# First layer of a two-layer transformer block: causal mask written by ScalarE into the scores' bank, and probabilities transposed into two PSUM banks by turns

## The chip, the cores and the metric

One core of a Trainium2 chip. The time is the device time of one execution in microseconds (us). The engines are named as in the profile: PE is TensorE (PEld its weight loads), DVE VectorE, ACT ScalarE, POOL GpSimd, SP SyncE, which here only issues DMAs.

## The reference, cut to what matters

Two layers run over x of shape (8, 256, 256); each adds an attention and a feed-forward branch to its input, both computed from the same layer norm. The change is in the first layer's attention, which is causal, with 16 query heads of width 16 and one key and value head:

```python
xn = _layernorm(x, axis=-1)
x = x + _L0_attn_ref(xn, ...) + _L0_ffn_ref(xn, ...)
# in _L0_attn_ref:
scores = jnp.einsum('bqhd,bkd->bhqk', q, k) * scale
causal = jnp.tril(jnp.ones((S, S), dtype=bool))
scores = jnp.where(causal[None, None], scores, min_val)
attn = jax.nn.softmax(scores, axis=-1)
ctx = jnp.einsum('bhqk,bkd->bqhd', attn, v)
```

The second layer has a full attention with 16 heads of width 128 and a mixture of 16 experts. The change does not touch it.

## The kernel before, in words

All work is in float32 held as a high and a low part (`fp32r`), so a product takes three matmuls: high by high, high by low, low by high. ACT writes the high part of a PSUM result, and DVE the low part behind it.

The first layer takes two sequences (512 tokens) at a time, in four turns. The attention of a turn is cut into 24 units, `units[g]`, 96 in all (`ALL`). A unit fills one PSUM bank (128 queries by 512 columns): for the first 128 queries of a sequence (`t` = 0) it holds four heads of 128 keys, and for the second 128 (`t` = 1) two heads of 256 keys. Each engine runs a written-out order of steps, `step(g)`:

- PE: `scores(g)`, `transposes(g-2)`, the items of `early[g]`, shared-expert work of `back_at[g]` (`shared`), `context(g-3)`, the items of `late[g]`. Items are the other products of the layer: `xT`, `q`, `kv`, `ffn`, `ctx`, `out`, `norm`. Here the shared expert belongs to the second layer and is done early.
- DVE: the row maxima of unit g (L791), the low part of the transposed probabilities of unit g-2 (L795), then its share of the items.
- ACT: `high_probs(g-2)` (L510), `exps(g)` (L502), then its share of the items.
- POOL: low parts of the hidden units and contexts, and in every step the splitting of a chunk of the second layer's weights, which SP stores and reloads.

`scores(g)` writes into `ps_s[g % 2]`. It begins with a product of the identity with the mask (L905), which writes minus 1e30 above the diagonal into the diagonal blocks (512 columns for `t` = 0, 256 for `t` = 1); one or two products of queries and keys (L907) are added onto it. It waits for the exponentials of unit g-2, which read the same bank.

`transposes(g)` turns the unit's probabilities in four 128x128 blocks (L916) into the one bank `ps_t`, ACT copies it out (L510), DVE takes the rest (L795), and only then may `transposes(g+1)` write `ps_t` again:

```python
pe.wait_ge(p_ok.sem, p_ok.at(0, g + 1))
pe.wait_ge(t_low.sem, t_low.at(0, g))
```

`context(g)` (L931 to L933) multiplies them with the values and waits for the low part of unit g. The bank `ps_b` serves the shared-expert items alone: ten of them per turn, placed in steps 8 to 16 and 23 of the turn after (in steps 8 to 17 for the third turn's; those of the last turn come behind the 96 steps). The last 18 steps of items are spread into the second layer.

Of the kernel before, what the change touches and what calls it, by code (L numbers as in the profile page):

```python
# [7 lines left out]
F32 = mybir.dt.float32  # L8
# [46 lines left out]
def stage_layer0(nc, ctx, dram):  # L55
# [40 lines left out]
    w_qkv = [sb(f"w_qkv{i}", [P, DC, D + P], R32) for i in range(2)]  # L96
    nc.sbuf_base += 4 * 4 * PC
    parts = [sb(f"parts{i}", [P, 2, PC], R32) for i in range(2)]
# [50 lines left out]
    raw_up = sb("raw_up_l0", [P, DC, HID], I32)  # L149
    mask_f = sb("mask_f", [P, P])  # L150
    assert nc.sbuf_base <= region_probs
# [101 lines left out]
    def stats_of(i):  # L253
        return TP + i

    qkv_parts = [(raw_qkv[:, :, 0:D], [w[:, :, 0:D] for w in w_qkv], HD0 ** -0.5),
                 (raw_qkv[:, :, D:D + P], [w[:, :, D:D + P] for w in w_qkv], 1.0),
# [13 lines left out]
    var_ok = sem("var_ok")  # L271
    zero_ok = sem("zero_ok")
    q3_rest = sem("q3_rest")
    cleared = sem("cleared")
# [144 lines left out]
    def gpsimd(pool):  # L419
        pool.memset(zeros[:], 0.0).then_inc(zero_ok, 1)  # L420
        pool.memset(ident[:], 0.0).then_inc(filled, 1)
        pool.memset(mask_f[:], 0.0).then_inc(filled, 1)
        pool.memset(minus_half[:], -0.5).then_inc(filled, 1)
        pool.wait_ge(filled, 3)
        pool.affine_select(out=ident[:], in_=ident[:], compare_op=ALU.not_equal, fill=1.0, base=0,
                           pattern=[[-1, P]], channel_multiplier=1).then_inc(const_ok, 1)
        pool.affine_select(out=mask_f[:], in_=mask_f[:], compare_op=ALU.is_ge, fill=MASKED, base=0,
                           pattern=[[-1, P]], channel_multiplier=1).then_inc(const_ok, 1)
# [65 lines left out]
    def scalar(act):  # L494
        act.sem_inc(p_ok.sem, 2)

        def exps(g):
# [7 lines left out]
            last.then_inc(p_ok.sem, 1)  # L505

        def high_probs(g):
            act.wait_ge(t_full.sem, t_full.at(0, g + 1))
            act.wait_ge(pv_ok.sem, pv_ok.at(0, g - 1))
            act.activation(pT[0][:, g % 2, :], ps_t[:], ACT.Copy).then_inc(t_high.sem, 1)  # L510

# [54 lines left out]
        for item in front:  # L566
            if item[0] == "q" and item[2] == 0:
                act.wait_ge(const_ok, 2)
                act.activation(ident_r[:], ident[:], ACT.Copy).then_inc(consts_r, 1)
                act.activation(mask_r[:], mask_f[:], ACT.Copy).then_inc(consts_r, 1)  # L570
                act.wait_ge(small_ok, 3)
                act.wait_ge(pads_zero, 2)
            early_item(item)
        def step(g):
# [30 lines left out]
            if LATE_AT <= g < LATE_AT + len(late_parts):  # L605
                raw, (high, _) = late_parts[g - LATE_AT]
                if g == LATE_AT:
                    act.wait_ge(late_in, 16 * LATE_LOADS)
                    act.wait_ge(pads_zero, 3)
                act.activation(high, raw, ACT.Copy).then_inc(late_high, 1)  # L610

        for g in range(ALL):
# [3 lines left out]
    def vector(dve):  # L616
# [170 lines left out]
        def step(g):  # L787
# [5 lines left out]
            if 2 <= g < ALL + 2:  # L793
                dve.wait_ge(t_high.sem, t_high.at(0, g - 1))
                dve.tensor_tensor(pT[1][:, g % 2, :], ps_t[:], pT[0][:, g % 2, :].bitcast(F32), ALU.subtract)\  # L795
                    .then_inc(t_low.sem, 1)
# [46 lines left out]
    def tensor(pe):  # L843
        pe.sem_inc(pv_ok.sem, 2)

        def product3(out, lhs, rhs, start, stop):
# [3 lines left out]
            return last  # L850

        def shared(p, n):

# [7 lines left out]
            if BACK[p][n] == ("sum", 0):  # L861
                pe.wait_ge(hs_low.sem, hs_low.at(0, len(ST) * (p + 1)))
            pe.wait_ge(b_done.sem, b_done.at(0, back_count(p, n) - (p == TURNS - 1 and n > 0)))
            out = back_bank(p, n)
            if kind == "ffs":
# [26 lines left out]
        def scores(g):  # L892
            p, s, t, j, nj = units[g]
            nh, w = DC * nj, (t + 1) * P
            out = ps_s[g % 2]
            if g == 0:
                pe.wait_ge(consts_r, 2)
            if t == 0 and j == 0:
                pe.wait_ge(item_done.sem, item_done.at(0, number["kv", p, s] + 1))
                pe.wait_ge(q3_got[s], 64 * (p + 1))  # L900
            if g == DC_HEADS // 4:
                pe.wait_ge(q3_rest, 64)
            pe.wait_ge(p_ok.sem, p_ok.at(0, g - 1))
            by_head = out[:].rearrange("p (h k) -> p h k", h=nh)
            pe.matmul(by_head[:, :, t * P:w], ident_r[:], mask_r[:].unsqueeze(1).to_broadcast([P, nh, P]), start=True, stop=False, skip_group_check=True)  # L905
            for a in range(nj):
                last = pe.matmul(out[:, a * DC * w:(a + 1) * DC * w].rearrange("p (c k) -> p c k", c=DC),  # L907
                                 q3[:, s, j + a, t * P:(t + 1) * P], k3[:, s, :, 0:w],
                                 start=False, stop=(a == nj - 1), skip_group_check=True)
            last.then_inc(s_full.sem, 1)  # L910

        def transposes(g):
            pe.wait_ge(p_ok.sem, p_ok.at(0, g + 1))
            pe.wait_ge(t_low.sem, t_low.at(0, g))
            for b in range(4):
                last = pe.transpose(ps_t[:, b * P:(b + 1) * P], probs[:, g % 3, b * P:(b + 1) * P], ident[:])  # L916
            last.then_inc(t_full.sem, 1)
# [1086 lines left out]
```

## Time and profile before

| | us |
|---|---|
| median of 3 runs | 1114.13 |
| lowest, highest | 1113.35, 1114.25 |
| the profiled execution's own time | 1113.54 |
| its span | 1111.8 |

The first layer's 96 steps run from 25 us to 372 us of the span, the second layer from there to the end. In rows of the timeline, the columns are start, duration, engine, line, operation, output and inputs; in brackets is the idle time of the engine before it and who ended it. Two operations in a row on one engine overlap in the records, so the start of the next is the better measure of what one costs. Times in the rows are microseconds unless marked otherwise.

### The profile page before, as it was taken

How to read it: one execution, taken by the hardware profiler on the slowest of the kernel's cores; microseconds unless marked ns; L12 is line 12 of the kernel's file. 1: busy time of each engine (PE TensorE's matmuls, PEld its weight loads, DVE VectorE, ACT ScalarE, POOL GpSimd, SP SyncE). 2: the span in 40 equal slices, each digit the busy share in tenths (PEclk: the TensorE clock that was granted, in tenths of full speed). 3: DMA queues.
4: the chain of work that ended last, by engine and by line, in shares of the span. 5: the costliest groups of instructions: out<-in, count | busy, mean ns of one | idle time of the engine just before them, and what ended most of it. 6: DMA issues, size and time to landing. Idle time of an engine off the chain costs nothing.

```text
span 1111.8 us, 21342 instructions
## 1 busy us (share of the span) xinstructions
PE 1046.6 (94%) x7339; PEld 956.7 (86%) x7339; DVE 840.2 (76%) x1696; ACT 687.6 (62%) x1922; POOL 519.5 (47%) x626
## 2 busy tenths in 40 slices
PE   8768899899899799999999999999999999999997
PEld 6657779779778688888899999999999999899997
DVE  6676787887867667887777777778777777777776
ACT  3856676766665435555666666766666665555554
POOL 5586665664675000007844454444453443588200
PEclk9999999999999999999999999999999999999999
DMA  7746746746664296624544554445445453333130
GB/s 219 230 129 193 215 142 204 202 153 190 176 211 138 91 261 175 220 87 157 173 139 139 150 203 148 149 134 158 161 140 177 147 163 99 106 100 97 65 114 19
DMA packets 140490, 171.71 MB, mean 154 GB/s; under 512 B 11232, under 2 KB 103520, under 8 KB 139488
## 3 DMA queue, kind: packets, MB, share of 16 engines
q1 hardware_dynamic: 137312, 161.96, 47.7%
q0 software_dynamic: 3072, 8.39, 2.3%
q8 instruction: 60, 0.98, 0.4%
q14 instruction: 46, 0.38, 0.1%
HBM read 121.95 MB, written 48.37 MB: 153 GB/s over the span
## 4 chain that ended last, share of the span: by engine, by line
PE 64%; DVE 13%; POOL 8%; ACT 6%; DMA 4%; issue 3%; SPq 2%; DVEq 0%; POOLq 0%; ACTq 0%
PE ps_m L1703 25%; PE ps_s L1703 9%; PE ps_t L1703 7%; PE ps_b L1703 4%; PE ps_b L849 3%; POOL d_xs L1332 3%; ACT probs L502 2%; PE ps_t L1858 2%; PE ps_c L1858 2%; PE ps_c L1703 2%; DMA d_w_head<-parts 2%; DVE neg_max L791 2%; PE ps_t L916 1%; PE ps_m L849 1%; DMA d_q_scr<-sT 1%
## 5 line engine op out<-in xcount | busy, mean ns | idle before, releaser
L1450 ACT ACTIVATE probs_a<-ps_s,neg_max_a 128x256 f32<-128x256 f32 x256 | 118.0, 473 | 139.6 <-DVE neg_max_a L1667 139.6
L1703 PE MATMUL ps_m<-xTa,w_qk 128*128 128x512 f32 x768 | 199.0, 398 | 4.2 <-DVE v L1519 1.6
L1703 PEld LDWEIGHTS ps_m<-xTa,w_qk 128*128 128x128 f32 x768 | 136.8, 188 | 34.7 <-issue 5.4
L502 ACT ACTIVATE probs<-ps_s,neg_max 128x128 f32<-128x128 f32 (+1 forms) x256 | 104.9, 422 | 55.4 <-DVE neg_max L791 54.2
L1667 DVE TENSOR_REDUCE neg_max_a<-ps_s 128x2 f32<-128x512 f32 x128 | 87.9, 690 | 43.3 <-PE ps_s L1703 41.7
L1349 POOL CAST we_down<-raw_down_e 128x256 fp32r<-128x256 f32 x47 | 18.7, 398 | 208.5 <-DMA raw_down_e<-in_we_down 208.5
L1703 PE MATMUL ps_m<-w_v,xTa 128*128 128x256 f32 x768 | 106.1, 288 | 0.0
L1703 PE MATMUL ps_s<-kTa,qTa 128*128 128x256 f32 x768 | 102.9, 283 | 0.3 <-DVE kTa L1489 0.2
L1703 PE MATMUL ps_t<-pTa,v 128*128 128x256 f32 x762 | 102.8, 284 | 0.0
L1703 PEld LDWEIGHTS ps_s<-kTa,qTa 128*128 128x128 f32 x768 | 96.7, 192 | 1.0 <-DVE kTa L1489 0.7
L1703 PEld LDWEIGHTS ps_t<-pTa,v 128*128 128x128 f32 x762 | 96.2, 191 | 0.1
L1703 PEld LDWEIGHTS ps_m<-w_v,xTa 128*128 128x128 f32 x768 | 95.9, 191 | 0.0
L1675 DVE TENSOR_TENSOR probs_a<-probs_a,ps_s 128x512 f32<-128x512 f32 x128 | 88.0, 687 | 4.4
L510 ACT ACTIVATE pT<-ps_t 128x512 fp32r<-128x512 f32 x96 | 57.8, 603 | 53.4 <-PE ps_t L916 52.5
L1345 POOL TENSOR_TENSOR we_up<-raw_up,we_up 128x704 fp32r<-128x704 f32 x47 | 80.4, 1710 | 1.9 <-ACT we_up L1392 1.8
L916 PE MATMUL ps_t<-ident,probs 128*128 128x128 f32 x384 | 58.8, 276 | 21.8 <-DVE pT L795 21.5
L1489 DVE SCALAR_TENSOR_TENSOR qTa<-ps_m,columns,qTa 128x512 fp32r<-128x512 f32 x64 | 47.9, 748 | 39.1 <-ACT qTa L1424 38.6
L1332 POOL DMA_INDIRECT d_xs<-rows_s,slot x32 | 31.5, 985 | 97.6 <-DVE slot L1561 88.2
L795 DVE TENSOR_TENSOR pT<-ps_t,pT 128x512 fp32r<-128x512 f32 x96 | 65.6, 683 | 13.7 <-ACT pT L510 13.2
L916 PEld LDWEIGHTS ps_t<-ident,probs 128*128 128x128 f32 x384 | 45.0, 141 | 32.8 <-issue 29.4
L1489 DVE SCALAR_TENSOR_TENSOR kTa<-ps_m,columns,kTa 128x512 fp32r<-128x512 f32 x64 | 48.0, 750 | 31.9 <-ACT kTa L1429 31.9
L1424 ACT ACTIVATE qTa<-ps_m,columns 128x512 fp32r<-128x512 f32 x64 | 44.2, 691 | 43.8 <-PE ps_m L1703 43.8
(261 smaller groups left out, 2827.9 us busy)
## 6 DMA issues: line engine op xcount, KB each, us to landing
w_qk<-d_w_head SPq DMA_DIRECT2D x64, 512.0 KB, 3.9
raw_up<-in_we_up SPq DMA_DIRECT2D x47, 352.0 KB, 3.6
d_w_head<-parts SPq DMA_DIRECT2D x128, 128.0 KB, 2.6
raw_down_e<-in_we_down SPq DMA_DIRECT2D x47, 256.0 KB, 2.9
codes<-in_w_codes SPq DMA_DIRECT2D x64, 128.0 KB
scales<-in_w_scales SPq DMA_DIRECT2D x64, 128.0 KB
q<-d_q_scr SPq DMA_DIRECT2D x28, 256.0 KB, 5.3
d_xs<-zeros SPq DMA_DIRECT2D x16, 384.0 KB, 5.6
```

The costliest lines, as they stand in the source:

```text
L502: last = act.activation(probs[:, g % 3, a * w:(a + 1) * w], ps_s[g % 2][:, a * w:(a + 1) * w], ACT.Exp, bias=neg_max[:, g % 2, a:a + 1], s ...
L510: act.activation(pT[0][:, g % 2, :], ps_t[:], ACT.Copy).then_inc(t_high.sem, 1)
L795: dve.tensor_tensor(pT[1][:, g % 2, :], ps_t[:], pT[0][:, g % 2, :].bitcast(F32), ALU.subtract)\
L849: last = pe.matmul(out, lhs[i], rhs[j], start=start and n == 0, stop=stop and n == 2, skip_group_check=True)
L916: last = pe.transpose(ps_t[:, b * P:(b + 1) * P], probs[:, g % 3, b * P:(b + 1) * P], ident[:])
L1332: pool.indirect_dma_start(dram["xs"], bass.IndirectOffsetOnAxis(ap=slots[k][:, t:t + 1], axis=0), rows[:, t, :], None).then_inc(sent, 16)
L1345: pool.tensor_tensor(we_up[1][:, b, :], raw_up[:, b, :], we_up[0][:, b, :].bitcast(F32), ALU.subtract).then_inc(up_ok, 1)
L1450: last = act.activation(probs[:, s, t, :], ps_s[s][:, t * SEQ:(t + 1) * SEQ], ACT.Exp, bias=neg_max[:, s, t:t + 1], scale=1.0, accum_out=s ...
L1489: dve.scalar_tensor_tensor(out=dst, in0=src, scalar=bias, in1=high.bitcast(F32), op0=ALU.add, op1=ALU.subtract).then_inc(signal, 1)
L1667: dve.tensor_reduce(neg_max[:, s, :], ps_s[s][:].rearrange("p (t k) -> p t k", t=2), AX.X, ALU.max, negate=True).then_inc(max_ok, 1)
L1675: dve.tensor_tensor(probs[:, s], probs[:, s], ps_s[s][:, 0:2].unsqueeze(2).to_broadcast([P, 2, SEQ]), ALU.mult)\
L1703: last = pe.matmul(out, lhs[i], rhs[j], start=start and n == 0, stop=stop and n == 2, skip_group_check=True)
```

## The change

A tile `mask_wide` of 128x256 takes the place of `mask_f` (128x128); its left half is zero and its right half is the mask. For every unit from the third on, ACT writes zeros and mask over the whole bank of scores, at the end of its step g-2, behind all items of that step. PE's mask product stays for the first two units only; from then on the products of queries and keys are added onto what ACT wrote. PE waits for `seeded` in place of `p_ok`.

Of the 48 odd units, 32 get `ps_b` as the bank for the transposes in place of `ps_t`: those whose step g+2 has no shared-expert item. A transpose then waits only for the last unit that used the same bank. Two waits come with it: transposes into `ps_b` wait for the shared-expert items before them (`b_done`), and these items wait for the last such transposes to be read (`t_low`).

```diff
+    second_bank = {g for g in range(1, ALL - 2, 2) if g + 2 not in back_at}
+    def turned_bank(g):
+        return ps_b if g in second_bank else ps_t
+    def turned_last(g):
+        return max((n for n in range(g) if (n in second_bank) == (g in second_bank)), default=-1)
+    def back_items(g):
+        return sum(BACK[p][n][0] != "close" for at, items in back_at.items() if at < g for p, n in items)
...
-        pool.memset(mask_f[:], 0.0).then_inc(filled, 1)
+        pool.memset(mask_wide[:], 0.0).then_inc(filled, 1)
...
+        def seed(g):
+            p, s, t, j, nj = units[g]
+            nh, w = DC * nj, (t + 1) * P
+            act.wait_ge(p_ok.sem, p_ok.at(0, g - 1))
+            act.activation(ps_s[g % 2][:].rearrange("p (h k) -> p h k", h=nh),
+                           mask_wide[:, 2 * P - w:2 * P].unsqueeze(1).to_broadcast([P, nh, w]), ACT.Copy).then_inc(seeded, 1)
         def high_probs(g):
...
-            act.activation(pT[0][:, g % 2, :], ps_t[:], ACT.Copy).then_inc(t_high.sem, 1)
+            act.activation(pT[0][:, g % 2, :], turned_bank(g)[:], ACT.Copy).then_inc(t_high.sem, 1)
...
                 act.activation(high, raw, ACT.Copy).then_inc(late_high, 1)
+            if g + 2 < ALL:
+                seed(g + 2)
...
-                dve.tensor_tensor(pT[1][:, g % 2, :], ps_t[:], pT[0][:, g % 2, :].bitcast(F32), ALU.subtract)\
+                dve.tensor_tensor(pT[1][:, g % 2, :], turned_bank(g - 2)[:], pT[0][:, g % 2, :].bitcast(F32), ALU.subtract)\
...
+        turned_until = {at: 1 + max((g for g in second_bank if g + 2 < step), default=-1) for step, items in back_at.items() for at in items}
         def shared(p, n):
...
+            pe.wait_ge(t_low.sem, t_low.at(0, turned_until[p, n]))
...
         # scores(g)
+            if g >= 2:
+                pe.wait_ge(seeded, g - 1)
...
-            pe.wait_ge(p_ok.sem, p_ok.at(0, g - 1))
             by_head = out[:].rearrange("p (h k) -> p h k", h=nh)
-            pe.matmul(by_head[:, :, t * P:w], ident_r[:], mask_r[:].unsqueeze(1).to_broadcast([P, nh, P]), start=True, stop=False, skip_group_check=True)
+            if g < 2:
+                pe.matmul(by_head[:, :, t * P:w], ident_r[:], mask_r[:].unsqueeze(1).to_broadcast([P, nh, P]), start=True, stop=False, skip_group_check=True)
...
         def transposes(g):
             pe.wait_ge(p_ok.sem, p_ok.at(0, g + 1))
-            pe.wait_ge(t_low.sem, t_low.at(0, g))
+            pe.wait_ge(t_low.sem, t_low.at(0, turned_last(g) + 1))
+            if g in second_bank:
+                pe.wait_ge(b_done.sem, b_done.at(0, back_items(g + 2)))
             for b in range(4):
-                last = pe.transpose(ps_t[:, b * P:(b + 1) * P], probs[:, g % 3, b * P:(b + 1) * P], ident[:])
+                last = pe.transpose(turned_bank(g)[:, b * P:(b + 1) * P], probs[:, g % 3, b * P:(b + 1) * P], ident[:])
```

## Rows read from the trace of the kernel before

**Rows 1.** The page's busy table: us, share of the span, instructions.

```profile
PE 1046.6 (94%) x7339; PEld 956.7 (86%) x7339; DVE 840.2 (76%) x1696; ACT 687.6 (62%) x1922; POOL 519.5 (47%) x626
```

**Rows 2.** Busy time in one window: PE, PEld, DVE, ACT, POOL, granted clock, DMA share, GB/s.

```profile
70.00:372.00 302.00, 274.31 (x1871) 242.83 (x1871) 229.21 (x464) 199.21 (x643) 183.13 (x230) 0.99 0.61 179
```

**Rows 3.** Waits in 70 to 372 us: total us, times, longest.

```profile
ACT pT L510 <- PE ps_t L916: 50.8, 47, 5.6
...
ACT probs L502 <- DVE neg_max L791: 45.3, 47, 2.5
...
PE ps_t L916 <- DVE pT L795: 11.7, 16, 1.7
```

**Rows 4.** The chain of waits that ended last, 36 to 107 us: start, us, what.

```profile
34.15 7.36 DMA d_w_head<-parts
...
68.66 1.15 POOL hT L455
```

**Rows 5.** Timeline of PE behind it.

```profile
70.06 1.21 PE L849 MATMUL ps_m<-w_o,cT 128*128 128x256 f32 x6 [1.78 <-POOL hT L455]
```

**Rows 6.** The mask products behind 70 us, by the view of line L905.

```profile
L905 PE MATMUL ps_s<-mask_r,ident_r x81: 277/283/562, 73.6 to 361.5; 128*128 128x256 f32 x56, 128*128 128x512 f32 x25
```

**Rows 7.** Timeline of PE: a short mask product, a late transpose, a wide mask product.

```profile
119.78 0.28 PE L905 MATMUL ps_s<-mask_r,ident_r 128*128 128x256 f32 x1
119.90 0.40 PE L907 MATMUL ps_s<-k,q 128*128 128x512 f32 x1
121.53 0.63 PE L916 MATMUL ps_t<-ident,probs 128*128 128x128 f32 x4 [1.23 <-DVE pT L795]
...
157.32 0.39 PE L905 MATMUL ps_s<-mask_r,ident_r 128*128 128x512 f32 x1
157.55 0.39 PE L907 MATMUL ps_s<-k,q 128*128 128x256 f32 x2
...
160.81 0.39 PE L849 MATMUL ps_b<-w_s,sT 128*128 128x256 f32 x1 [1.51 <-DVE sT L688]
```

**Rows 8.** The chain of waits: first and last mask product in it behind 70 us.

```profile
73.83 0.36 PE ps_s L905
...
343.52 0.12 PE ps_s L905
```

**Rows 9.** The same chain at the end of the second turn, through DMAs.

```profile
175.25 4.73 DMA d_q_scr<-sT
...
182.75 5.36 DMA d_w_head<-parts
```

**Rows 10.** The same chain just before the late transpose.

```profile
119.85 0.33 DVE xn1T L661
120.19 0.60 DVE neg_max L791
120.78 0.61 DVE pT L795
```

**Rows 11.** Timeline of ACT, a copy of 512 columns from SBUF and one from PSUM.

```profile
159.10 0.64 ACT L529 ACTIVATE sT<-gated_s 128x512 fp32r<-128x512 f32 x1
159.62 0.40 ACT L597 ACTIVATE ctx_raw<-ps_c 128x256 f32<-128x256 f32 x1
159.88 0.62 ACT L510 ACTIVATE pT<-ps_t 128x512 fp32r<-128x512 f32 x1
```

**Rows 12.** Timeline where PE is closest behind ACT's end of a step: ACT, then PE.

```profile
92.21 0.41 ACT L582 ACTIVATE cT<-ctx_f 128x256 fp32r<-128x256 f32 x1
92.70 0.60 ACT L510 ACTIVATE pT<-ps_t 128x512 fp32r<-128x512 f32 x1
...
93.20 0.28 PE L905 MATMUL ps_s<-mask_r,ident_r 128*128 128x256 f32 x1
```

**Rows 13.** Groups of POOL, 0 to 30 us: busy us, mean ns, idle before.

```profile
L420 POOL MEMSET zeros<- 128x256 f32 x1 | 0.3, 312 | 0.3 <-POOLq L1992 0.3
...
L422 POOL MEMSET mask_f<- 128x128 f32 x1 | 0.2, 209 | 0.0
```

More of the change, by code:

```diff
@@ L96, in stage_layer0 @@
     w_qkv = [sb(f"w_qkv{i}", [P, DC, D + P], R32) for i in range(2)]
-    nc.sbuf_base += 4 * 4 * PC
+    mask_wide = sb("mask_wide", [P, 2 * P])
+    nc.sbuf_base += 4 * (4 * PC - 2 * P)
     parts = [sb(f"parts{i}", [P, 2, PC], R32) for i in range(2)]
@@ L149, in stage_layer0 @@
     raw_up = sb("raw_up_l0", [P, DC, HID], I32)
-    mask_f = sb("mask_f", [P, P])
     assert nc.sbuf_base <= region_probs
@@ L272, in stage_layer0 @@
     zero_ok = sem("zero_ok")
+    seeded = sem("seeded")
     q3_rest = sem("q3_rest")
@@ L426, in gpsimd @@
                            pattern=[[-1, P]], channel_multiplier=1).then_inc(const_ok, 1)
-        pool.affine_select(out=mask_f[:], in_=mask_f[:], compare_op=ALU.is_ge, fill=MASKED, base=0,
+        pool.affine_select(out=mask_wide[:, P:2 * P], in_=mask_wide[:, P:2 * P], compare_op=ALU.is_ge, fill=MASKED, base=0,
                            pattern=[[-1, P]], channel_multiplier=1).then_inc(const_ok, 1)
@@ L569, in scalar @@
                 act.activation(ident_r[:], ident[:], ACT.Copy).then_inc(consts_r, 1)
-                act.activation(mask_r[:], mask_f[:], ACT.Copy).then_inc(consts_r, 1)
+                act.activation(mask_r[:], mask_wide[:, P:2 * P], ACT.Copy).then_inc(consts_r, 1)
                 act.wait_ge(small_ok, 3)
```

## The prediction

> **What bounds the kernel now.** I read the page's busy table first, then the busy time of windows, the waits, the chain of waits, and the timeline of single steps. Over the whole span PE is busiest, with 94% [rows 1]. The change lies in the first layer, so its part of the span is what counts, and that part has two stretches.
>
> Up to 70 us the chain runs through DMAs and POOL, which splits weight chunks: it enters a DMA at 34.15 and leaves POOL at 69.8 with a low part of a hidden unit [rows 4]. PE then has stood idle for 1.78 us and starts the first output product at 70.06 [rows 5]. What PE gains before that is lost again in this wait.
>
> From 70 to 372 us PE is busy for 274.3 of 302 us (91%), DVE for 229.2 (76%), ACT for 199.2 (66%) [rows 2]. ACT mostly waits: 47 times for transposes (50.8 us) and 47 times for row maxima (45.3 us). PE waits 16 times for DVE before a transpose, 11.7 us in all [rows 3]. The reader should see an array that is nearly full, but whose order is tied to DVE and ACT by short waits, so the chain changes engine all the time. A microsecond less on PE is not a microsecond less at the end.
>
> **Part 1: the mask products go.** Behind 70 us there are 81, of them 56 of 256 columns and 25 of 512 [rows 6]. Their cost is the time to the start of the next matmul: 119.90 - 119.78 = 0.12 us and 157.55 - 157.32 = 0.23 us [rows 7]. PE loses 56 x 0.12 + 25 x 0.23 = 12.5 us of work. The extra time of the first matmul behind a transpose stays, since the product of queries and keys inherits it. That is the upper end. The lower end is what the chain holds: 22 of the 81 are on it, the first with 0.36, three with 0.23 and 18 with 0.12, together 3.2 us [rows 8]. Others were beside the chain when they ran, but mostly on a path hardly shorter. In some stretches the array does not matter: at the end of a turn the chain passes a DMA of 4.73 us, SP's queue and a DMA of 5.36 us, 12.9 us from 175.25 to 188.1, and something alike one turn later [rows 9]. I take the middle, 7.8 us.
>
> The 13 products before 70 us (units 2 to 14) count as nothing, covered by POOL's chain.
>
> The matmul durations themselves can mislead here. The window gives PE 91% by matmuls and 242.8 of 302 us, 80%, by weight loads [rows 2]. The Trainium skill (Perfetto Trace Analysis, "Identifying the Most-Contended Engine") says that matmul busy time is no good measure of how full TensorE is, since matmuls are pipelined, and that the share of weight loads should be read. By its reading the array would have a fifth of its time free, barely less than DVE's quarter, and the lower end of this part would be the right one; that is the second rival.
>
> **Part 2: the transposes alternate.** Two thirds of the odd units go to `ps_b`, so a transpose beside them no longer waits for the DVE pass of the unit just before. At most the 11.7 us of rows 3 come back, at least nothing. In rows 7 the transpose waited 1.23 us, because DVE worked without a pause before it: values, normed tokens, maxima, low part [rows 10]. That work remains. PE can now do the transpose and the item behind it earlier, but `context` in the same step still wants the same low part, and the next scores want ACT's seed. I take a third, 4 us. Late next is DVE itself.
>
> The new waits: shared-expert items wait for the low part of a unit three or more steps back, which the `context` behind them wants anyway. The first transpose into `ps_b` behind a group of such items waits for DVE to have read the last one. That can cost up to one DVE pass of 0.6 us at five places; I take it at nothing, as PE does a `context` and the scores in between, and keep 0 to 3 us.
>
> **Part 3: ACT writes the seeds.** The trace has no ACT write into a PSUM bank from SBUF. Next to it are a copy of 512 columns from SBUF (0.64 us, next start after 0.52 us) and one from PSUM (0.62 us) [rows 11]. I take 0.52 us in a full queue, bounded by 0.45 and 0.65. The 81 seeds behind 70 us are 42 us of ACT, against 302 - 199.2 = 103 us that it stands idle. So the throughput holds, at (199 + 42) / 302 = 80%. What matters is order. The seed of unit g+2 stands behind all of ACT's items of step g and ahead of the copy of the transposes of unit g-1 and of the exponentials of unit g+1; DVE's low parts and PE's contexts wait behind those. Where ACT reached the copy L510 and had to wait for PE (47 of 83 times, units 13 to 95), the seed fits into the wait, mostly. In the other 36 it pushes everything behind it by up to 0.52 us: at most 18.7 us. At least nothing: all twelve times that the chain enters L510 behind 70 us it comes from PE's transposes, never from ACT's own previous work. Then there are ACT's tails that PE waits for, as the 1.51 us before the shared expert's second product [rows 7]: a seed ahead of them lengthens them. I take a quarter of the upper end, 4.5 us, nearer to the chain's zero.
>
> Before, `scores(g+2)` waited for the exponentials of step g, now for the seed behind the whole step. Queued behind this wait are all of PE's later work. Behind 70 us the closest case is PE at 93.20 with ACT through its step at 92.62, 0.58 us [rows 12]; a seed of 0.6 us just misses it by 0.1 us, and no other margin there is under 0.85 us. But where part 2 lets PE run ahead, this margin is what stops it, a further reason for only a third.
>
> Before 70 us the seeds of units 2 to 14 are 13 x 0.52 = 6.8 us of ACT. PE's 1.78 us [rows 5] cover them and the gaps do the rest: nothing. If that cover is gone, up to 6.8 - 1.8 = 5 us come on top; a gain is excluded there as POOL's chain holds the end of the stretch.
>
> **Small edits.** The mask tile's memset doubles in width, 0.1 us more [rows 13], once, ahead of the identity, while the input is still loading: nothing. No DMA is added or moved. The second layer is the same.
>
> **Sum.** 7.8 + 4.0 - 4.5 = 7.3 us off. The profiled execution took 1113.54, its span 1111.8 with 1.7 us around it; that gives 1106.2. The median of the runs is 0.6 higher and would give 1106.8. I say 1106.5.
>
> **The rivals.**
>
> First, slower: ACT's queue becomes the bound. Place: the steps in which ACT goes from item to copy without a pause. Price: 0.52 us each. It decides once more than (7.8 + 4.0) / 0.52 = 23 of the 81 seeds show up at the end, with 36 candidates. With 30 of them and 2 us from the stretch before 70 us it is 15.6 + 2 - 11.8 = 5.8 us slower, about 1119; with all, and 5 us, 1125. For it: ACT's outputs feed DVE in every item, and DVE is second busiest. Against it: 103 us of idle ACT time, and the chain never passes a step's end on ACT.
>
> Second, no change: the array was not the limit. The chain's 3.2 us go, the alternating banks only move the wait from the transposes to `context`, and the seeds cost 3: 1113.3. For it: only 22 of 81 mask products on the chain, and the reading of weight loads. Against it: ACT waits for the transposes of a late PE for 50.8 us.
>
> Third, much faster: everything on PE counts, 12.5 + 11.7 - 4.5 = 19.7 us: 1094. For it: in many steps PE has no gap at all. Against it: rows 9 and 10.
>
> **How the numbers follow.** My forecast 0.56 (own range 1102 to 1110), slower 0.19, no change 0.15, much faster 0.10. A measurement of this kernel tells 0.2%, 2.2 us, from no change. Faster by more is 0.56 + 0.10 = 0.66, within it 0.15, slower 0.19. The range must reach into both sides: 1097 leaves out about half of the third rival and 1118 some more than half of the first, together less than 0.2.
>
> **What would show it right or wrong.** Part 1: L905 with 2 matmuls in place of 96, and PE's busy time from 70 us on down by about 12 us. Part 2: PE's wait for DVE before L916 down from 11.7 us to a few, and new waits of `context` (L931) for L795 that are smaller than what went. Part 3: a new ACT group of 94 with about 0.6 us each; PE waiting for it before L907 under 3 us in all. The first rival would show L510 and L502 with little idle time before them, and PE waiting for ACT's group or for DVE work behind it for more than 10 us. The second would show PE's busy share lower by the 12 us and the steps as long as before. Wrong altogether would be a first output product later than 70 us by more than a microsecond, or a second layer of another length.

## The result, and the profile after

| | before | after |
|---|---|---|
| median, 11 runs each, side by side | 1113.09 us | 1116.35 us |
| lowest | 1111.58 us | 1113.35 us |
| the profiled execution, its span | 1113.54, 1111.8 us | 1120.17, 1118.4 us |

The changed kernel is slower: ratio 1.0033, 95% interval 1.002 to 1.0045, so 2.2 to 5.0 us of 1113. The forecast was 1106.5, faster; the result lies inside the range of 1097 to 1118. (One run of the changed kernel took 1670.49 us at a granted clock of 0.56 and is not counted.) The profiled execution is near the slow end of its kernel's runs, so single microseconds of it are checked below against a second profile of the same kernel, e9.

The busy table of the changed kernel (us, share of the span, instructions), to be laid beside [rows 1]:

```profile
PE 1043.3 (93%) x7245; PEld 951.0 (85%) x7245; DVE 839.8 (75%) x1696; ACT 733.6 (66%) x2016; POOL 520.3 (47%) x626
```

PE has 94 instructions fewer, ACT 94 more, DVE and POOL the same work. The window behind the first output product, in the columns of [rows 2], and then four stretches of it:

```profile
70.00:377.00 307.00, 270.05 (x1795) 237.54 (x1793) 231.18 (x467) 239.73 (x731) 183.58 (x231) 0.97 0.60 176
78.40:81.60 3.20, 3.15 (x13) 2.56 (x13) 2.54 (x5) 2.82 (x8) 2.88 (x5) 0.50 0.58 150
102.40:105.40 3.00, 2.89 (x14) 2.61 (x13) 1.62 (x3) 2.97 (x13) 2.76 (x4) 0.50 0.31 102
221.80:224.80 3.00, 3.00 (x10) 2.42 (x10) 1.47 (x3) 1.50 (x5) 2.76 (x5) 0.50 0.26 84
314.00:317.00 3.00, 3.00 (x14) 2.72 (x13) 1.52 (x3) 1.43 (x3) 2.84 (x5) 0.50 0.34 108
```

The same in the kernel before, for two of these stretches:

```profile
221.00:225.00 4.00, 4.00 (x25) 3.35 (x24) 3.09 (x5) 3.02 (x10) 3.58 (x5) 1.00 0.31 84
314.00:317.00 3.00, 3.00 (x19) 2.63 (x19) 1.98 (x3) 1.60 (x6) 2.80 (x5) 1.00 0.44 128
```

Three readings. In this execution the last of the first layer's transposes starts at 374.1 us in place of 369.4. In e9, the same kernel in an execution near the fast end of its runs (1144.73 us, median 1147.56), it starts at 368.0, so one trace does not say where the 3 us between the medians are lost. The engine that was relieved, PE, now stands idle for 307 - 270.1 = 37 us in place of 27.7 [rows 2], and DVE for 76 in place of 73. And the granted clock, which the prediction left out, is 0.50, the level of 1.2 GHz, in pieces of about 3.4 us (begins at 78.3, 102.2, 221.6, 313.8 and 371.8, together 17 us behind 70; before, one piece of 3.4). PE got less done in them: 10 matmuls in 3.0 us against 25 in 4.0 in one stretch, 14 against 19 in 3.0 us in the other, not of the same sizes. What it did before the first of them is in the timeline of PE; the waits are in brackets:

```profile
69.00 0.44 PE L1018 MATMUL ps_m<-ident,rinv_wide 128*128 128x128 f32 x2 [1.27 <-ACT rinv_wide L613]
...
70.63 0.95 PE L874 MATMUL ps_m<-w_o,cT 128*128 128x256 f32 x6 [0.50 <-POOL hT L470]
...
77.39 1.16 PE L994 MATMUL ps_m<-ident,xn 128*128 128x128 f32 x6 [2.10 <-DVE xn L678]
78.23 0.54 PE L963 MATMUL ps_c<-pT,v_wide 128*128 128x256 f32 x1
78.57 0.42 PE L964 MATMUL ps_c<-pT,v_wide 128*128 128x256 f32 x1
```

A context matmul that takes 0.28 us at full clock takes 0.42 from 78.57 on. In the ten microseconds before, PE had stood idle for 1.27 + 0.50 + 2.10 = 3.9 us.

ACT's new group (busy us, mean ns, idle before), and the timeline of two steps of ACT:

```profile
L527 ACT ACTIVATE ps_s<-mask_wide 128x512 f32<-128x512 f32 x94 | 57.3, 609 | 1.0
```

```profile
60.26 0.60 ACT L527 ACTIVATE ps_s<-mask_wide 128x512 f32<-128x512 f32 x1
60.80 0.58 ACT L533 ACTIVATE pT<-ps_b 128x512 fp32r<-128x512 f32 x1
```

The next operation starts 0.54 us after the seed; over the 70 seeds with no pause behind them the median is 0.52, the price that was forecast. The waits, first from 28 to 70 us, then from 70 to 378 (total us, times, longest):

```profile
PE ps_s L937 <- ACT ps_s L527: 7.5, 7, 2.7
```

```profile
ACT probs L517 <- DVE neg_max L816: 34.0, 40, 2.8
...
DVE pT L820 <- ACT pT L533: 15.6, 30, 1.3
...
ACT pT L533 <- PE ps_t L948: 13.1, 16, 2.0
...
ACT pT L533 <- PE ps_b L948: 10.3, 8, 1.9
...
PE ps_b L874 <- DVE sT L713: 5.0, 3, 2.0
PE ps_b L874 <- DVE xn1T L686: 4.2, 2, 2.3
PE ps_b L874 <- DVE gated_s L718: 4.1, 4, 1.5
PE ps_m L1018 <- ACT rinv_wide L613: 3.9, 4, 1.2
...
PE ps_m L1018 <- DVE gated L698: 3.3, 2, 2.3
PE ps_c L963 <- DVE pT L820: 3.2, 4, 1.4
...
PE ps_s L937 <- ACT ps_s L527: 0.9, 2, 0.7
```

The six rows on `ps_b`, `ps_m` and `ps_c`, items and contexts that wait for DVE and ACT, are 23.7 us together. Before, in 70 to 372 us, four of them were there already, with 10.2 us, and no context waited for a low part:

```profile
PE ps_b L849 <- DVE sT L688: 4.2, 3, 1.5
PE ps_b L849 <- DVE gated_s L693: 2.6, 4, 1.0
...
PE ps_b L849 <- DVE xn1T L661: 2.4, 2, 1.3
...
PE ps_m L986 <- DVE gated L673: 1.0, 2, 0.7
```

So PE's wait of 11.7 us ahead of the transposes [rows 3] is all but gone, and 13.5 us of other waits for DVE and ACT have come in its place (11.4 in e9, where the six rows are 21.6). The seeds hold PE up in the first stretch, 7 times for 7.5 us, and hardly behind it.

### The profile page after: what moved, and what is told of

It is laid out like the page before. It is cut to its first block, busy times and chain, and to the rows that moved or that the text cites. A ratio compares the mean times of both kernels' runs of the same rounds, so it can differ in the third digit from the quotient of the medians.

```text
span 1118.4 us, 21276 instructions
## 1 busy us (share of the span) xinstructions
PE 1043.3 (93%) x7245; PEld 951.0 (85%) x7245; DVE 839.8 (75%) x1696; ACT 733.6 (66%) x2016; POOL 520.3 (47%) x626
## 4 chain that ended last, share of the span: by engine, by line
PE 61%; DVE 11%; POOL 10%; ACT 6%; DMA 5%; issue 4%; SPq 3%; POOLq 0%; DVEq 0%; ACTq 0%
PE ps_m L1735 25%; PE ps_s L1735 9%; PE ps_t L1735 6%; PE ps_b L1735 3%; POOL d_xs L1364 3%; PE ps_b L874 3%; ACT probs L517 2%; DMA d_w_head<-parts 2%; PE ps_t L1890 2%; PE ps_c L1890 2%; PE ps_c L1735 2%; DMA d_q_scr<-sT 1%; PE ps_m L874 1%; POOL codes L464 1%; POOL parts L462 1%
## 5 line engine op out<-in xcount | busy, mean ns | idle before, releaser
L1461 ACT ACTIVATE kTa<-ps_m,columns 128x512 fp32r<-128x512 f32 x64 | 44.1, 688 | 41.0 <-PE ps_m L1735 40.9
L963 PE MATMUL ps_c<-pT,v_wide 128*128 128x256 f32 x192 | 60.8, 316 | 7.0 <-DVE pT L820 5.6
L816 DVE TENSOR_REDUCE neg_max<-ps_s 128x2 f32<-128x512 f32 (+1 forms) x96 | 65.3, 681 | 2.1 <-PE ps_s L937 2.0
L1448 ACT ACTIVATE v<-ps_m 128x512 fp32r<-128x512 f32 x64 | 38.3, 599 | 38.0 <-PE ps_m L1735 38.0
```

The lines of the kernel that those rows point to most:

```text
L816: dve.tensor_reduce(neg_max[:, g % 2, 0:nh], ps_s[g % 2][:].rearrange("p (h k) -> p h k", h=nh), AX.X, ALU.max, negate=True).then_inc(max_ ...
L963: pe.matmul(out, vh, high, start=first, stop=False, skip_group_check=True)
```

## The experiments

There were eighteen runs, e5 and e9 of kernels already known. Each ratio is against the kernel before on the same chip. In the groups e1 to e4, e9 to e12 and e16 to e18 that kernel has a median of 1143 to 1145 us: on those chips every kernel, the one before too, loses some 30 us between about 510 and 560 us, in the second layer. Spans are not compared across the two kinds of chips; starts in the first layer are, but each is from one execution, and the two of the kernel before differ by 0.6 us, the two of the changed kernel by 6.1.

| | ratio, 95% interval | last transpose starts | what it is |
|---|---|---|---|
| after | 1.0033, 1.002 to 1.0045 | 374.1 | the change |
| e9 | 1.0024, 1.0012 to 1.0035 | 368.0 | the change again |
| e1 | 1.0024, 1.0013 to 1.0035 | 369.6 | seeds, one bank |
| e2 | 1.0019, 1.0004 to 1.0033 | 371.0 | two banks, mask products |
| e3 | 1.0023, 1.0013 to 1.0032 | 369.1 | two banks, no mask |
| e4 | 1.0025, 1.0012 to 1.0038 | 369.5 | the change, products of zeros |
| e5 | one run, 1112.15 against 1112.97 | 368.8 | before again |
| e6 | 1.0002, 0.9991 to 1.0013 | 366.7 | one bank, no mask |
| e7 | 0.9952, 0.9937 to 0.9968 | 363.4 | before, half maxima |
| e8 | 0.9966, 0.9955 to 0.9978 | 362.1 | the change, half maxima |
| e10 | 1.0036, 1.0022 to 1.005 | 371.7 | the change, two products of zeros |
| e11 | 0.9899, 0.9885 to 0.9912 | 359.1 | before, no maxima |
| e12 | 0.9894, 0.9876 to 0.9912 | 356.2 | the change, no maxima |
| e13 | 1.029, 1.0269 to 1.0311 | 398.3 | the change, seeds early |
| e14 | 0.993, 0.9918 to 0.9942 | 361.9 | two banks, half maxima |
| e15 | 1.0007, 0.9996 to 1.0017 | 371.2 | two banks, PE kept busy early |
| e16 | 1.0007, 0.9994 to 1.002 | 368.2 | e6 with products of 16 columns |
| e17 | 1.0015, 1.0004 to 1.0026 | 374.2 | the change with them |
| e18 | 0.9993, 0.9982 to 1.0004 | 366.6 | e8 with them |

### The parts one by one: e1, e2, e3, e5, e6

e1 keeps the seeds and puts every transpose into `ps_t`; e2 keeps the two banks and takes the mask from PE again; e3 is e2 without any mask from the third unit on, e6 the same with one bank. e6 is thus part 1 of the prediction alone, and e5, the kernel before unchanged, is its counterpart on the same chip. In e3 and e6 the causal mask is missing from the result, which changes the numbers and not the amount of work behind them. The diffs of e1 to e4, e6, e8, e10 and e12 to e18 are against the changed kernel, those of e7 and e11 against the one before.

```diff
e1, e6:
-    second_bank = {g for g in range(1, ALL - 2, 2) if g + 2 not in back_at}
+    second_bank = set()
e2, e3, e6:
-            if g + 2 < ALL:
-                seed(g + 2)
...
-                pe.wait_ge(seeded, g - 1)
+            pe.wait_ge(p_ok.sem, p_ok.at(0, g - 1))
e2:
-            if g < 2:
+            if True:
e3, e6:
-                                 start=False, stop=(a == nj - 1), skip_group_check=True)
+                                 start=(g >= 2 and a == 0), stop=(a == nj - 1), skip_group_check=True)
```

> The changed kernel with all transposes in ps_t: ACT's seeds without the second bank. Theory (A): ACT's seeds delay its copies and exponentials, and the freed array time comes back as idle time and as stretches at the lower clock; then this is slower than the kernel before as the changed kernel is, about 1116 to 1119 us. Rival (B): the seeds are harmless and the new bank with its waits costs; then this is about 1106 us.

> The kernel before with the transposes in two banks by turns; PE's mask products stay, ACT writes no seeds. Theory (A): PE's waits for DVE before L916 (22 us in all) fall to a few, some of it comes back at context, and the time falls by 1 to 4 us, to about 1110. Rival (B): the new waits cost, about 1117 us or more.

> Two banks by turns, no mask product from the third unit on and no seed either: the causal mask is left out of the computation there. It shows what the freed array time is worth without ACT's part. Theory (A): the array's relief is real where ACT doesn't stand in the way, 1103 to 1108 us. Rival (C), less work on the array only brings idle time and more stretches at the lower clock, whatever ACT does: 1113 us or more, with four or more stretches at half clock between 70 and 380 us as in the changed kernel.

> No mask product from the third unit on, no seed, one bank (the causal mask is left out of the computation there): the array's relief of 12 us alone. Theory (E), DVE's chain and the tails behind it set the pace of the first layer: within 2 us of the kernel before, and the relief stands in the trace as idle time of PE before products that wait for DVE. Rival (D), the array sets the pace and it was the second bank's waits that took the relief away in the run without mask before: 6 to 12 us faster.

> The kernel before, once more, for its trace on the chip of this group: the first layer's 96th scores near 361 us, as in its first trace, if what this chip adds lies in the second layer alone.

Removing the mask products alone changes nothing that can be measured (1.0002). Two banks alone cost 2.1 us (0.0019 x 1113, interval 0.4 to 3.7). The seeds cost 2.5 us, as the difference of e1 and e6, which ran on different chips. Added up, 0.2 + 2.1 + 2.5 = 4.8 us, against 3.7 measured for all and 2.7 for e9, within the intervals. But where two banks are there already, the seeds add less: 0.1 us (e9 less e3) to 1.1 us (the change less e3), and 0.3 us between e4 and e2, which have PE's work alike and ran on one chip. The medians of e1 to e4, all of that chip, lie within 1.0 us (1145.95 to 1146.93). So either part costs 2 to 3 us by itself, and both together hardly more; the shares of a sum are not shown. Taking the mask away altogether with two banks (e3) is no better than keeping it (e2).

The same window in e5 (before again) and e6:

```profile
70.00:372.00 302.00, 274.63 (x1875) 243.30 (x1876) 230.49 (x466) 200.23 (x648) 183.21 (x231) 0.99 0.61 179
```

```profile
70.00:370.00 300.00, 264.51 (x1798) 232.35 (x1796) 229.25 (x468) 200.58 (x650) 183.51 (x231) 0.99 0.62 180
```

PE lost 10.1 us of work and the first layer 2.1 us (366.7 against 368.8), in one execution each. The other 8 turned into idle time of PE, 35.5 us against 27.4, while DVE's idle time stayed at 71. The longest row of PE's waits, e5 and then e6, in the same window, has 4.8 of the 8 us:

```profile
PE ps_t L916 <- DVE pT L795: 10.8, 15, 1.7
```

```profile
PE ps_t L945 <- DVE pT L818: 15.6, 21, 1.9
```

The 2.1 us were then lost in the second layer: from the last transposes to the end it takes 744.3 us in e6 and 741.6 in e5. In e6's timeline of the second layer POOL splits an expert's weights late, because they come late (6.5 us after they were asked for at 650.27):

```profile
656.85 0.40 POOL L1378 CAST we_down<-raw_down_e 128x256 fp32r<-128x256 f32 x1 [10.31 <-DMA raw_down_e<-in_we_down]
```

and in its chain of waits:

```profile
650.27 6.53 DMA raw_down_e<-in_we_down
```

In e5 the same transfer, the longest of the three between 640 and 664 us, took 4.7 us. Between 560 and 1000 us PE waits for the weights twice in e6, 2.0 us in all, and not once in e5.

In e2 the alternating banks let PE get ahead and then stand before the first output product; the timeline of PE, then a window of it:

```profile
66.67 0.48 PE L1015 MATMUL ps_m<-ident,rinv_wide 128*128 128x128 f32 x2 [1.69 <-ACT rinv_wide L613]
...
71.19 1.62 PE L872 MATMUL ps_m<-w_o,cT 128*128 128x256 f32 x6 [2.75 <-POOL hT L470]
...
75.17 0.63 PE L932 MATMUL ps_s<-mask_r,ident_r 128*128 128x512 f32 x1
```

```profile
67.00:77.00 10.00, 7.25 (x33) 6.89 (x33) 3.27 (x7) 1.85 (x10) 9.27 (x13) 0.50 0.55 155
```

The clock falls to half for 10.2 us, from 66.9 on; the 16th scores start at 75.6 us in place of 74.0 (73.2 in e5).

### Work given back to PE: e4, e9, e10

e4 puts a product with zeros where the mask product stood, e10 two, e9 is the changed kernel.

```diff
+            if g >= 2:
+                zero_half = v_wide[:, 0:P // 2].unsqueeze(1).unsqueeze(1).to_broadcast([P, nh, 2, P // 2])
+                pe.matmul(by_head[:, :, t * P:w].rearrange("p h (a k) -> p h a k", a=2), ident_r[:], zero_half, start=False, stop=False, skip_group_check=True)
```

> The changed kernel with a product of the identity and zeros, as large as the old mask product, added onto every seed: ACT's part as in the changed kernel, the array's work as before. If the array's relief of 12 us still reaches the end (rival D), this is 6 to 12 us slower than the changed kernel, 1122 us or more. If ACT's queue sets the pace and the relief only turned into idle time (A), it is within 2 us of the changed kernel, and if the stretches at half clock come from that idle time, there are fewer of them here and the time is the same or up to 3 us less, 1113 to 1117 us.

> The changed kernel once more, for its time and trace on one chip with the run below: 3 to 4 us slower than the kernel before, with 15 us or more of the first layer at half clock.

> The changed kernel with two products of the identity and zeros added onto every seed, each as large as the old mask product: 25 us more work on the array than in the changed kernel, 12 more than before. Theory (E), the array doesn't set the pace: within 3 us of the changed kernel, with fewer stretches at half clock, and the array's idle time gone. Rival (D), the array is the bound: 15 us slower or more than the changed kernel.

With all its mask work back on the array the changed kernel is as slow as without (1.0025 and 1.0024, on two chips). Twice that work, some 25 us by the prices of the prediction and 18.6 of busy time by the windows below, adds 1.4 us to the median on the same chip (1148.93 against 1147.56), and the intervals overlap. Windows of e9 and e10:

```profile
70.00:371.00 301.00, 265.62 (x1796) 234.09 (x1796) 229.71 (x467) 240.62 (x733) 183.82 (x231) 0.99 0.61 180
```

```profile
70.00:374.00 304.00, 284.24 (x1960) 254.24 (x1960) 230.68 (x467) 240.87 (x733) 184.42 (x232) 1.00 0.61 179
```

PE's idle time goes from 35.4 to 19.8 us, DVE's from 71.3 to 73.3. e10 has no piece at half clock behind 70 us, e9 has two, and e10 is not faster for it; so the clock is not the main part of the loss, though the added work stands against it here.

### DVE relieved: e7, e8, e11, e12, e14

In e7 and e8 the row maxima run over the first half of each row, in e11 and e12 they are left out; e14 is e7 with two banks.

```diff
e7 (e8 and e14 alike):
-                dve.tensor_reduce(neg_max[:, g % 2, 0:nh], ps_s[g % 2][:].rearrange("p (h k) -> p h k", h=nh), AX.X,
+                dve.tensor_reduce(neg_max[:, g % 2, 0:nh], ps_s[g % 2][:].rearrange("p (h k) -> p h k", h=nh)[:, :, 0:256 // nh], AX.X,
e11, e12:
-            act.wait_ge(max_ok.sem, max_ok.at(0, g + 1))
+            act.wait_ge(s_full.sem, s_full.at(0, g + 1))
...
-                dve.tensor_reduce(neg_max[:, g % 2, 0:nh], ps_s[g % 2][:].rearrange("p (h k) -> p h k", h=nh), AX.X,
-                                  ALU.max, negate=True).then_inc(max_ok.sem, 1)
...
+        dve.memset(neg_max[:], 0.0).then_inc(max_ok.sem, 1)
```

> The kernel before with the row maxima taken over the first half of each head's keys: 96 DVE passes of 0.68 us become about 0.42 us, 25 us less on DVE and 0.26 us less between the scores and the exponentials of each unit; PE's work is the same. Theory (E): 5 to 15 us faster. Rival (D), the array at 91% is the bound: 2 us or less.

> The changed kernel with the same shorter row maxima. Theory (E): now the array is nearer to being the bound, and its relief of 12 us begins to show: faster than the kernel before with shorter maxima by 2 us or more. Theory (A), ACT's queue is what the seeds fill: no faster than that one, or slower by up to 5 us.

> The kernel before without its 96 row maxima in the first layer (the exponentials take the scores as they are): 65 us less on DVE and 0.75 us less from scores to exponentials. Theory (E), DVE sets the pace as far as the array lets it: 8 to 18 us faster than before, with the array above 95% busy from 70 us on. If ACT's queue were the pace (A), within 3 us of the kernel with half maxima.

> The changed kernel without the row maxima. Theory (E) with ACT's part small: now the array is the bound and its relief of 12 us shows, 5 to 12 us faster than the kernel before without maxima. Theory (A), the seeds fill ACT's queue: within 2 us of that one, or slower.

> Two banks by turns, PE's mask products, no seeds, row maxima over half the keys. If the second bank only moves waits and costs 2 us by half clock (E), about 1.002 of the kernel before with half maxima, or 0.997 of before. If it helps once DVE has room, faster than that kernel, 0.993 of before or less.

The window of e7, then of e14:

```profile
70.00:366.00 296.00, 273.54 (x1871) 242.77 (x1871) 208.41 (x463) 197.32 (x643) 183.50 (x231) 0.99 0.63 182
```

```profile
70.00:365.00 295.00, 273.65 (x1875) 244.52 (x1876) 207.52 (x463) 196.62 (x643) 184.32 (x231) 0.99 0.63 183
```

22 us less of DVE's work brings 5.6 us at the end (1107.38 against 1112.97), and with the maxima gone 10.9 (1133.93 against 1144.78), where 10 us less of PE's work brought nothing. So DVE, with what waits for it, sets more of the pace than PE at 91%; but a fourth comes back, not all, so no engine is the bound alone. The edit also brings each unit's exponentials closer to its scores, and no run tells that from DVE's load. With DVE relieved the two banks may help: e14 has the best ratio of the kernels that still take maxima, 0.993, ahead of e7 (the intervals overlap by 0.0005, on different chips). Its maxima can be smaller than the rows' true ones, which leaves the softmax as it is, since a shift cancels, and costs headroom against overflow. The whole change with half maxima (e8) ends its first layer 1.3 us before e7 and is slower all the same: its second layer takes 744.1 us, e7's 742.0. Without any maxima the sign turns: on one chip the change (e12) has a median 1.7 us under the kernel before (e11, 1132.24 against 1133.93) and ends its first layer 2.9 us earlier. The ratios, 0.9894 and 0.9899, have overlapping intervals, and the 5 to 12 us that were expected did not come.

### The order on ACT and the clock: e13, e15

e13 issues the seed right behind the exponentials, ahead of the step's items. e15 is e2 with four products of zeros in each scores of units 5 to 14, meant to leave PE no long pause before 70 us.

```diff
e13:
...
+            if g + 2 < ALL:
+                seed(g + 2)
...
-            if g + 2 < ALL:
-                seed(g + 2)
e15:
+            if 5 <= g < 15:
+                ...
+                for _ in range(4):
+                    pe.matmul(by_head[:, :, t * P:w].rearrange("p h (a k) -> p h a k", a=2), ident_r[:], zero_half, start=False, stop=False, skip_group_check=True)
```

> The changed kernel with each seed right behind the exponentials of its step instead of behind the step's items. The scores no longer wait for ACT's items, but every item's high part comes up to 0.5 us later, and DVE's low part behind it. If the wait of PE for the seeds is what costs, 2 to 4 us faster than the changed kernel, level with before or better; if the delay of ACT's items for DVE is what costs, 2 us slower than the changed kernel or more.

> The two banks alone, with four products of the identity and zeros more in each of the units 5 to 14: 6 us of array work in a stretch where PE stood idle for 8 us. If the half clock behind that idle time is what costs (clock), no stretch at half clock from 60 to 80 us, the 16th scores at 74 us or earlier instead of 75.6, and 1 to 2 us less than the two banks alone: 1.000 to 1.001 of before. If not, as slow as the two banks alone or up to 3 us slower, 1.002 to 1.005.

e13 loses 2.9%, 32 us against 3.7: the largest effect of all from one instruction moved within a step. Its waits from 70 to 400 us:

```profile
ACT probs L517 <- DVE neg_max L816: 49.5, 53, 2.4
...
POOL cT L484 <- ACT cT L607: 47.2, 12, 7.5
...
DVE gated L698 <- ACT gated L570: 30.8, 18, 2.7
```

In the same window the changed kernel has 34.0, 39.2 and 19.0 us in these rows. The seed now stands ahead of the step's items, on which DVE and POOL wait, so these come up to a seed's 0.54 us later. PE stands idle for 330 - 275.6 = 54 us and DVE for 100, and e13 has 27.3 us at half clock behind 70, the changed kernel 17; what part of the 28 us between them is the clock is not measured. e15 still has a pause and a piece at half clock, in the timeline and the window:

```profile
70.63 0.95 PE L872 MATMUL ps_m<-w_o,cT 128*128 128x256 f32 x6 [2.54 <-POOL hT L470]
```

```profile
71.70:75.00 3.30, 3.30 (x17) 3.20 (x16) 0.87 (x3) 0.00 (x0) 2.98 (x5) 0.50 0.39 113
```

That is 3.4 us at half clock in place of 10.2 there, the 16th scores at 74.3 in place of 75.6, and 1.0007 in place of 1.0019. But two more pieces follow, at 102.3 and 221.7 us, so both kernels have 13.7 us of half clock up to 370 us, and the last transpose starts at 371.2 as against 371.0. The intervals overlap, and e14 has 10.2 us at half clock from 65.6 on and is fast all the same. Whether the clock is a part of what two banks cost is not shown.

### What happens in the second layer: e16, e17, e18

In e6, e8, e13 and the changed kernel, none of which has mask products from the third unit on, the second layer takes 744.1 to 744.3 us; in those with them on like chips (before, e5, e7, e14, e15) 741.6 to 742.7. PE's waits for expert weights (`we_up`, from 560 to 1000 us) split the same way: 0.9 to 3.4 us in the eight kernels without a product there, 0 to 0.7 in the nine with one. There is one more sign of it: from the point that e5 reaches at 649 us to the one that it reaches at 680 us, the eight take 1.2 to 1.6 us longer than e5, the nine 0 to 0.4, on both kinds of chips. Three kernels put a product of 16 zero columns in its place (in e16 with start on, since no seed stands in the bank).

```diff
+            if g >= 2:
+                pe.matmul(out[:, 0:16], ident_r[:], v_wide[:, 0:16], start=False, stop=False, skip_group_check=True)
```

> The kernel with one bank, the seed order of before and no mask on anything from the third unit on (its output lacks the mask), with a product of 16 zero columns put where each mask product stood: PE's instruction list is as long as before, its work is not. Theory A (the missing instructions shift something in the second layer, so that its weights come late): the first layer ends near 366.7 to 367.5 us as without the product, the second layer is 741.5 to 743 us long in place of 744.3, PE waits for the expert weights (we_up) under 0.8 us in place of 2.0, and the ratio is 0.997 to 0.999. Theory B (what counts is when the first layer's work ends or how much PE does in it): the second layer stays near 744 us with waits of 1.5 us or more, and the ratio is 1.000 to 1.001.

> The changed kernel with the same product of 16 zero columns ahead of the products of queries and keys, from the third unit on. Theory A: the second layer is 741.5 to 743 us long in place of 744.3, and the ratio is about 1.001. Theory B: second layer near 744 us, ratio 1.003.

> The changed kernel with row maxima over the first half of each row and the same product of 16 zero columns. Without the product its first layer ended at 362.1 us, earlier than that of the kernel before with half maxima (363.4), and its second layer took 744.1 us in place of 742.0. Theory A: 362 + 742, ratio 0.993 to 0.995, no worse than two banks with half maxima (0.993). Theory B: ratio 0.9965 as before.

The waits for `we_up` are gone in e16 and e18, and 0.6 us in e17, and none of the three is slower than e5 between the two points: the split now holds in twenty traces. It does not go by the end of the first layer (366.7 us in e6, with 2.0 us of waits, 374.2 in e17, with 0.6). But whether it goes by the number of PE's instructions or by their work these runs do not tell, since the small product is not cheap. PE's timeline in e6, then in e16:

```profile
141.39 0.39 PE L934 MATMUL ps_s<-k,q 128*128 128x512 f32 x1
141.62 0.60 PE L945 MATMUL ps_t<-ident,probs 128*128 128x128 f32 x4
```

```profile
141.45 0.17 PE L934 MATMUL ps_s<-v_wide,ident_r 128*128 128x16 f32 x1
141.48 0.48 PE L936 MATMUL ps_s<-k,q 128*128 128x512 f32 x1
141.80 0.60 PE L947 MATMUL ps_t<-ident,probs 128*128 128x128 f32 x4
```

The product of queries and keys starts 0.03 us behind the small one but takes its place for 0.32 us in place of 0.23, so the scores cost 0.35 us in place of 0.23: 16 columns cost as much as the 256 of a short mask product, 0.12 us [rows 7]. The window shows it too, 6.4 of the 10.1 us that e6 took from PE are back:

```profile
70.00:370.00 300.00, 270.91 (x1871) 240.67 (x1871) 229.44 (x466) 199.83 (x648) 183.97 (x231) 0.99 0.61 180
```

The forecast of the time was wrong: the ratios are 1.0007, 1.0015 and 0.9993, against 0.997 to 0.999, 1.001 and 0.993 to 0.995. e18 is even slower than e8, with a first layer 4.5 us longer. These three ran on a chip of the slower kind, where the second layer's length (773.5 us in e16) is no longer split by the products (772.3 to 774.6 with, 773.4 to 775.0 without). That the waits are real and where they come from is shown; that they are what cancels e6's 2.1 us fits e5 and e6 alone. Why a transfer comes late stays open. One rival is the loading of instructions: a transfer of the page's instruction queue falls into e6's late one and none into e5's. But one also falls into e14's and into e15's, which took 4.9 us each, so that alone does not do it.

## Why the prediction was wrong

| step | forecast | measured |
|---|---|---|
| part 1, mask products | 7.8 us off | 0.2 us more, interval 1.0 off to 1.4 more (e6) |
| part 2, two banks | 4.0 us off | 2.1 us more (e2) |
| part 3, seeds | 4.5 us more | about 2.5 us more with one bank (e1 less e6), 0.1 to 1.1 with two |
| sum | 7.3 us off | 3.7 us more |

**Part 1 failed, and decided the sign.** The lower end, the 3.2 us that the chain of waits held [rows 8], was right in kind: 2.1 us at the end of the first layer. The step that failed is "Others were beside the chain when they ran, but mostly on a path hardly shorter ... I take the middle". The work of the other 59 mask products came back as slack: 8 of the 10 us became idle time of PE. Their work was oversized as well, 12.5 us against 10.1. The Trainium skill (Perfetto Trace Analysis, "Identifying the Most-Contended Engine") says to judge TensorE's headroom by the share of weight loads and by the share of peak arithmetic, and not by matmul busy time. The share of weight loads was 80% [rows 2], and e6 agrees in kind; the second rival, which followed it, was a microsecond off for the end of the first layer (3.2 against 2.1). That even the 2.1 us do not reach the end was in no rival.

**Part 2 had the wrong sign.** "At most the 11.7 us of rows 3 come back, at least nothing" was no lower bound. The wait did go, as forecast, and 13.5 us of others came in its place, of which the prediction named the contexts (3.2 us) but not the items (10.3 us). "That work remains", said of DVE, was the right sentence, and it should have set the value at nothing: what PE no longer waits for in the transposes it waits for one product later. What takes it below nothing stays open. PE running ahead into a pause of 2.75 us and 10 us at half clock (e2) is the candidate, and e15 does not bear it out.

**Part 3 was right in kind, oversized, and in part in another place.** The price of a seed was right (0.52 us), the throughput held, PE's wait for it behind 70 us is 0.9 us, under the 3 said. In the first stretch "the gaps do the rest: nothing" was wrong in its detail: PE waited there 7.5 us for seeds. Most of that was covered; the first output product came 0.57 us late, within the microsecond named. The first rival, ACT as the bound, had the sign right. One half of its mark, over 10 us of PE's waits for ACT's group, fails with 0.9 behind 70. The other half, waits for DVE work behind the seeds, can't be told in the changed kernel from the waits that part 2 moved; in e1, which has the seeds alone, PE waits 19.5 us for the low parts, in e6 15.6. e13 shows how much the order on ACT can cost.

**The clock was missing.** The profiled execution of the changed kernel has 17 us at half clock behind 70 us, before 3.4. Half of the difference, 6.8 us, would be lost if PE were the bound throughout; e9 has only 6.8 us of such pieces there, and e5, the kernel before, 3.4. So the clock may explain why that profile is at the slow end of its runs; its share in the 3.7 us is not measured.

**The second layer** "of another length" was named as a sign of something altogether wrong, and it came: 744.3 in place of 742.4 us, with 1.2 us of it between the two points above.

## What to carry to other kernels

An engine busy for 91% is not a bound: ask whose idle time stays the same when others change, and price removed work nearer to what the chain of waits holds of it (3.2 us here, 2.1 measured at the layer's end) than to a middle (7.8). A wait that is removed while the work behind it stays is worth nothing until something shows who is late next; relieving DVE by 22 us gave 5.6, and PE by 10 us nothing. An instruction added to an engine that feeds two others goes behind what they wait for: the place of the same 94 writes within the step was worth 28 us (e13 less the change). And a filler that is to keep the number of instructions without their work has to be priced first.

## What was not expected of the hardware

- The granted clock drops to 0.50 for 3.4, 6.8 or 10.2 us at a time in kernels in which PE is busy for over 90% of the window, mostly behind or in waits of PE of one to three microseconds (2.10 us before 78.3 in the changed kernel, 1.91 before 101.0 in e6). How much of it there is between 25 and 370 us differs between two executions of one kernel (6.8 and 10.2 us of the one before, 20.5 and 17.1 of the changed one) and does not simply follow PE's work: 6.8 in e10, 10.2 in e6, 13.7 in e15, 27.3 in e3.
- ACT writes 128x512 from SBUF into a PSUM bank in 609 ns on average, about as fast as it copies from PSUM to SBUF (600 ns), and in this kernel matmuls with start off then add onto it, in banks that a product with start on had begun once.
- A product of 16 columns ahead of another adds 0.12 us to the two, as much as one of 256 columns, 0.12 (e16 against e6 and the kernel before).
- Whether 94 products more stand on PE in the first layer decides whether PE waits for expert weights 290 us and more behind it (0.9 to 3.4 us without, 0 to 0.7 with, in twenty traces).
- On some chips all kernels lose about 30 us at one place of the second layer, in and around 31 to 34 us at a granted clock of one half. The changed kernel has 1.0033 on the one kind and 1.0024 on the other.
